# Graph layers on one core: block buffers per graph, key sums taken from w's two parts, t1 and t2 loaded behind the g blocks

## The chip, the cores and the metric

One core of a Trainium2 chip runs the whole problem in one launch. The metric is the time of an execution on the device in microseconds; the median of the runs is compared.

## What is computed

64 graphs of 256 nodes and 512 features pass through two layers in fp32. x and adj are also handed over transposed, and Wv and W1 transposed.

```python
h = jnp.maximum(_layernorm(x, axis=-1), 0.0)
# layer 0, attention weighted by adj
weight = adj * jnp.exp(einsum('bqd,bkd->bqk', h @ Wq.T + bq, h @ Wk.T + bk))
weight = weight / jnp.sum(weight, axis=2, keepdims=True)
x = x + einsum('bqk,bkd->bqd', weight, h @ Wv.T + bv)
# layer 1
h = jnp.maximum(_layernorm(x, axis=-1), 0.0)
agg = einsum('bij,bjf->bif', adj, h) / jnp.maximum(deg, EPS)
x = x + relu(concat([h, agg]) @ W.T)
```

## The kernel before

Graphs are worked in 32 pairs; a pair is 512 rows, four tiles of 128. Each engine has its own program, and semaphores with constant or counted targets bind them. After a first step and step 1 a loop runs steps 2 to 30, then come `last_step` and `final_step`. Step i does layer 0 of pair i and layer 1 of pair j = i - 1, interleaved.

fp32 products are made of three fp32r matmuls (`product`, L514): high by high, high by low, low by high. So every operand X is kept as `X_h` (ACT copies it, L813 to L886) and `X_l` (X minus `X_h`, on POOL or DVE).

PE's step (L660), in order: `kp` (four tiles of the combined query-key projection), `v` tile 0, `scores` of both graphs, `v` 1 to 3; then `strassen` products of layer 1 with weights B11, B21, T1, T2, T3, T4, B22 (p = 0 to 6, two row rounds each), with `az` (adj times z) between them; `sum_weights` (L601: a matrix of ones times the weights' sums over key tiles, so that every partition holds the sum of each query); and four `av`.

Several things share a place. `n_h`/`n_l` hold the kp weights, and, in the middle of a step, t1 and t2 (products 2 and 3): SP loads these after kp (`load_t`, L284) and loads n back after the products (`load_n`, L289). `w` holds adj, then the exponentials and weights of pair i, then u3 and ha1. g_full's memory is that of `g_h` and `g_l`: parts A11, A12 and S4 of h, and u2. All eight PSUM banks are in use and named at L52 to L56.

h must be transposed. DVE turns 32x32 blocks (`turn`, L1072) into `blocks`, SP stores `blocks` to HBM, waits, and loads it back in another order as `turned` (`load_turned`, four DMAs per graph). There is one `blocks` tile, so the second graph's turn waits for the first one's store (L1078, L1085). This happens twice per step: g (layer 1, pair j) and h (layer 0, pair i+1).

DVE ends a step with `sum_ha0`, `layer1_result` for tiles 0 to 3 (y at L1223, then x at L1227) and `sum_inverses` (L1243) before the fourth; then `finish_layer0`. PE's av(t) waits for y of tile t - 1 (L710 to L715), whose bank it takes. POOL's and ACT's last work of a step is hT_h and hT_l of the next pair, then at_h and at_l.

```python
            def sum_weights(i, dst):
                pe.wait_ge(sum_split, i + 1)
                every, all_ones = bank[dst][:, :], ones[:, 0:1].to_broadcast([P, P])
```

## Time and profile before

| | |
|---|---|
| median of 3 runs | 1941.86 us (1937.01 to 1943.64) |
| profiled execution | 1942.48 us, span 1940.4 us |
| PE | busy 98% of the span, 8956 matmuls, mean granted clock 0.996 |
| PE weight loads | 81% |
| DVE, POOL, ACT | 81%, 57%, 44% |
| DMA | 370.7 MB, 191 GB/s |

A row of the timeline gives start, duration, engine and line of an instruction, then what it writes and reads. PE's rows overlap, since a matmul is given with its way through the array; the distance between two starts is what one costs. In the page "idle before" is time in which an engine stood still before an instruction, with what released it.

### The profile page before, as it was taken

How to read it: one execution, taken by the hardware profiler on the slowest of the kernel's cores; microseconds unless marked ns; L12 is line 12 of the kernel's file. 1: busy time of each engine (PE TensorE's matmuls, PEld its weight loads, DVE VectorE, ACT ScalarE, POOL GpSimd, SP SyncE). 2: the span in 40 equal slices, each digit the busy share in tenths (PEclk: the TensorE clock that was granted, in tenths of full speed). 3: DMA queues.
4: the chain of work that ended last, by engine and by line, in shares of the span. 5: the costliest groups of instructions: out<-in, count | busy, mean ns of one | idle time of the engine just before them, and what ended most of it. 6: DMA issues, size and time to landing. Idle time of an engine off the chain costs nothing.

```text
span 1940.4 us, 29261 instructions
## 1 busy us (share of the span) xinstructions
PE 1892.7 (98%) x8956; PEld 1576.8 (81%) x8956; DVE 1579.6 (81%) x2649; ACT 862.4 (44%) x1453; POOL 1103.0 (57%) x1066
## 2 busy tenths in 40 slices
PE   8899999999999999999999999999999999999997
PEld 5778888888888888888788888888888888887885
DVE  6887888888788888888878888887888878888776
ACT  4344444444444445443445443444444454434442
POOL 4665565565565565655655655655655656546552
PEclk9999999999999999999999999999999999999999
DMA  6456656566656566555566555566555665555632
GB/s 222 148 189 212 210 181 196 188 203 207 210 178 190 198 205 204 192 198 173 189 208 219 188 194 184 191 211 211 179 191 194 204 203 194 197 173 184 211 125 87
DMA packets 190881, 370.69 MB, mean 191 GB/s; under 512 B 17936, under 2 KB 115216, under 8 KB 182672
## 3 DMA queue, kind: packets, MB, share of 16 engines
q1 hardware_dynamic: 190864, 370.48, 57.2%
q8 instruction: 9, 0.15, 0.0%
q14 instruction: 8, 0.07, 0.0%
HBM read 266.60 MB, written 103.81 MB: 191 GB/s over the span
## 4 chain that ended last, share of the span: by engine, by line
PE 49%; DVE 19%; DMA 17%; issue 8%; SPq 4%; POOL 2%; ACT 1%; DVEq 1%; POOLq 0%; ACTq 0%
PE bank L518 16%; PE bank L520 16%; PE bank L519 16%; DMA turned_store<-blocks 8%; DMA n_l<-t_store 8%; DVE y L1223 3%; SPq L263 3%; DVE x L1235 3%; DVE stats L1091 2%; DVE x L1227 2%; DVE g_full L1213 2%; DVE deg L1112 1%; DVE mean_sum L1096 1%; DVE blocks L1073 1%; DVE sums L1252 1%
## 5 line engine op out<-in xcount | busy, mean ns | idle before, releaser
L403 POOL TENSOR_TENSOR hT_l<-turned,hT_h 128x512 fp32r<-128x512 f32 x122 | 181.9, 1517 | 264.0 <-ACT hT_h L824 263.9
L242 POOL TENSOR_TENSOR w_l<-w,w_h 128x512 fp32r<-128x512 f32 x62 | 80.3, 1295 | 307.5 <-ACT w_h L857 307.5
L1073 DVE STREAM_TRANSPOSE blocks<-h 128x512 f32<-128x512 f32 x252 | 163.3, 685 | 110.3 <-DMA turned_store<-blocks 110.3
L518 PE MATMUL bank<-hT_h,n_h 128*128 128x512 f32 x512 | 200.9, 392 | 3.9 <-DVE hT_l L1164 2.8
L519 PE MATMUL bank<-hT_l,n_h 128*128 128x512 f32 x512 | 200.2, 391 | 0.0
L520 PE MATMUL bank<-hT_h,n_l 128*128 128x512 f32 x512 | 200.2, 391 | 0.0
L518 PE MATMUL bank<-wv_h,hT_h 128*128 128x512 f32 x512 | 199.6, 390 | 0.0
L519 PE MATMUL bank<-wv_l,hT_h 128*128 128x512 f32 x512 | 199.5, 390 | 0.0
L520 PE MATMUL bank<-wv_h,hT_l 128*128 128x512 f32 x512 | 199.3, 389 | 0.0
L399 POOL TENSOR_TENSOR xb<-x_in,bv_b 128x512 f32<-128x512 f32 x128 | 165.9, 1301 | 43.5 <-DVE x L1235 39.3
L843 ACT ACTIVATE kz_h<-bank,kp_bias 128x512 fp32r<-128x512 f32 x128 | 83.6, 675 | 207.5 <-PE bank L520 207.5
L518 PE MATMUL bank<-hT_h,kz_h 128*128 128x256 f32 x512 | 146.3, 286 | 5.0 <-DVE kz_l L1158 5.0
L519 PE MATMUL bank<-mix_l,g_h 128*128 128x512 f32 x384 | 149.4, 389 | 0.0
L518 PE MATMUL bank<-mix_h,g_h 128*128 128x512 f32 x384 | 149.4, 389 | 0.0
L520 PE MATMUL bank<-mix_h,g_l 128*128 128x512 f32 x384 | 149.4, 389 | 0.0
L818 ACT ACTIVATE h<-x,rs 128x512 f32<-128x512 f32 x124 | 94.4, 809 | 117.0 <-POOL rs L393 117.0
L520 PE MATMUL bank<-hT_h,kz_l 128*128 128x256 f32 x512 | 145.6, 284 | 0.0
L519 PE MATMUL bank<-hT_l,kz_h 128*128 128x256 f32 x512 | 145.6, 284 | 0.0
L1227 DVE SCALAR_TENSOR_TENSOR x<-y,x 128x512 f32<-128x512 f32 x124 | 141.7, 1143 | 4.3
L1123 DVE CUSTOM_DVE_ANT_0 h<-h,u_b,bqk 128x512 f32<-128x512 f32 x128 | 121.4, 968 | 0.0
L518 PE MATMUL bank<-n_h,hT_h 128*128 128x512 f32 x256 | 103.1, 403 | 18.3 <-DMA n_l<-t_store 15.9
L387 POOL TENSOR_TENSOR rs<-var_eps,minus_half 128x2 f32<-128x2 f32 x128 | 90.0, 703 | 50.8 <-DVE var_eps L1101 44.5
(152 smaller groups left out, 5394.9 us busy)
## 6 DMA issues: line engine op xcount, KB each, us to landing
turned_store<-blocks SPq DMA_DIRECT2D x126, 512.0 KB, 4.5
turned<-turned_store SPq DMA_DIRECT2D x504, 128.0 KB, 2.9
x_in<-x SPq DMA_DIRECT2D x32, 1024.0 KB, 5.3
n_h<-t_store SPq DMA_DIRECT2D x31, 1024.0 KB, 6.3
n_l<-t_store SPq DMA_DIRECT2D x31, 1024.0 KB, 8.3
...
```

The costliest lines, as they stand in the source:

```text
L242: engine.tensor_tensor(w_l[:, g], w[:, g], w_h[:, g].bitcast(F32), ALU.subtract).then_inc(w_split, 1)
L387: pool.tensor_tensor(rs[n][:, 0, tiles], var_eps[n][:, tiles], minus_half[:, :], ALU.pow).then_inc(rstd_done[n], 1)
L399: pool.tensor_tensor(xb[:, t, :], x_in[:, t, :], bv_b[:, :], ALU.add).then_inc(xb_done, 1)
L403: pool.tensor_tensor(by_blocks(hT_l, t), turned_tile(t), by_blocks(hT_h, t).bitcast(F32), ALU.subtract).then_inc(hT_split, 1)
L518: pe.matmul(dst, lh, rh, start=first, stop=False, skip_group_check=more)
L519: pe.matmul(dst, lh, rl, start=False, stop=False, skip_group_check=more)
L520: mm = pe.matmul(dst, ll, rh, start=False, stop=last, skip_group_check=more)
L818: nc.scalar.activation(h[:, t, :], src[:, t, :], ACT.Relu, bias=rs[n][:, 1, t:t + 1], scale=rs[n][:, 0, t:t + 1]).then_inc(h_done[n], 1)
L843: nc.scalar.activation(kz_h[:, dt, :], bank[KP_BANK[dt]][:, :], ACT.Identity, bias=kp_bias[:, dt:dt + 1]).then_inc(kp_high, 1)
L1073: nc.vector.transpose(blocks[:, :, :, t % NT, :].rearrange("p j c b -> p c j b"), h[:, t, :].rearrange("p (c j b) -> p c j b", c=DT, b=Q)) ...
L1123: nc.vector.tensor_tensor_reduce(h[:, t, :], h[:, t, :], u_b[:, :], 1.0, bqk[:, 0:1], ALU.mult, ALU.add, key_bias[:, t:t + 1]).then_inc(ke ...
L1227: nc.vector.scalar_tensor_tensor(out=place[:, t, :], in0=y[:, :], scalar=0.0, in1=place[:, t, :], op0=ALU.max, op1=ALU.add).then_inc(x2_do ...
```

## The change

It does six things.

- `blocks` becomes two tiles, one for each graph. A turn waits for the last store of its own tile. On DVE both turns of g stand after the first and second kp split, the degrees behind the kp splits, both turns of h before sum_z.
- SP stores g block 0, issues x_in, stores g block 1, and then loads both. t1 and t2 come behind them in two halves with a semaphore each; PE waits for each half before its own product. `reload_n` puts n_l behind h's store, and h's loads follow when layer 1's parts are made (`parts_made`).
- p0's copies (`z_sum`) move from a tile of their own to g_full's first quarters, the place of A11 and later S4. ACT therefore writes S4 only once z's low parts are made (`z_split`).
- `sum_weights` takes four matmuls, `w_h` and `w_l` by two key tiles, in place of two from `sum_h` and `sum_l`. The pair adds, `high_sum` and `low_sum` go. PE runs them after az(1), in bank 6, instead of after az(3), in bank 7; DVE's `sum_inverses` stands before `sum_ha0`.
- Banks: kp(3) takes 3, v(0) and v(1) 7 and 3, av(0) and av(1) 7 and 1. PE waits for sum_inv before kp(1).
- At the ends W1's feature half is loaded as soon as x1 and the bias sums allow, n's store comes late in the first step, low_mix(T2) stands before hT_l, and the last pair's sum_z and low_z stand before combine_s4 and the degrees.

```diff
-KP_BANK, V_BANK, SCORE_BANK = (5, 6, 2, 7), (3, 7, 0, 1), (0, 1)
-AZ_BANK, AV_BANK, SUM_BANK = (1, 0, 4, 2), (3, 1, 0, 4), 7
+KP_BANK, V_BANK, SCORE_BANK = (5, 6, 2, 3), (7, 3, 0, 1), (0, 1)
+AZ_BANK, AV_BANK, SUM_BANK = (1, 0, 4, 2), (7, 1, 0, 4), 6
...
             wz_raw = (g_full[:, 0], g_full[:, 1])
+            z_sum = (g_full[:, 0, 0, :], g_full[:, 1, 0, :])
             u2 = (g_full[:, 0, 1, :], g_full[:, 1, 1, :])
...
-        blocks = sb("blocks", [P, Q // 8, DT, NT, Q])
+        blocks = [sb(f"blocks{g}", [P, Q // 8, DT, NT, Q]) for g in range(G)]
...
             engine.tensor_tensor(w_l[:, g], w[:, g], w_h[:, g].bitcast(F32), ALU.subtract).then_inc(w_split, 1)
-            engine.wait_ge(w_split, G * i + g + 1)
-            engine.tensor_tensor(w[:, g, 0, :], w[:, g, 0, :], w[:, g, 1, :], ALU.add).then_inc(w_summed, 1)
...
                 sp.dma_start(turned_d[k, g].rearrange("i a j n -> (i a) (j n)"),
-                             blocks[:, :, :, :, :].rearrange("p j c t b -> p (j c t b)")).then_inc(stored[g], 16)
+                             blocks[g][:, :, :, :, :].rearrange("p j c t b -> p (j c t b)")).then_inc(stored[g], 16)
...
-            def move_h(i):
+            def move_g(j, between=None):
+                store_blocks(1, 0, g_turned, T * j + NT, g_stored)
+                if between is not None:
+                    between()
+                store_blocks(1, 1, g_turned, T * (j + 1), g_stored)
                 for g in range(G):
-                    store_blocks(0, g, h_turned, T * (i - 1) + NT * (g + 1), h_stored)
-                    sp.wait_ge(h_stored[g], 16 * i)
-                    load_turned(0, g, h_moved)
-            def move_g(j):
-                for g in range(G):
-                    store_blocks(1, g, g_turned, T * j + NT * (g + 1), g_stored)
                     sp.wait_ge(g_stored[g], 16 * (j + 1))
                     load_turned(1, g, g_moved)
+            def parts_made(j, g):
+                sp.wait_ge(*((combined, 4 * (j + 1)) if g == 0 else (part_split, 7 * j + A22)))
...
-            def load_t(i):
-                sp.wait_ge(kp_psum, DT * (i + 1))
-                sp.dma_start(n_h[:, :, :].bitcast(F32), t_d[0]).then_inc(t_loaded, 16)
-                sp.dma_start(n_l[:, :, :].bitcast(F32), t_d[1]).then_inc(t_loaded, 16)
-            def load_n(j, p):
-                half = slice(2 * (p - 2), 2 * (p - 1))
-                sp.wait_ge(p_psum, PER_PAIR * j + products_done(p, 1))
+            def load_t(k):
+                half = slice(2 * k, 2 * k + 2)
+                sp.dma_start(n_h[:, half, :].bitcast(F32), t_d[0, :, half, :]).then_inc(t_loaded[k], 16)
+                sp.dma_start(n_l[:, half, :].bitcast(F32), t_d[1, :, half, :]).then_inc(t_loaded[k], 16)
+            def reload_n(j, k, h_blocks):
+                half = slice(2 * k, 2 * k + 2)
+                sp.wait_ge(p_psum, PER_PAIR * j + products_done(2 + k, 1))
                 sp.dma_start(n_h[:, half, :].bitcast(F32), n_d[0, :, half, :]).then_inc(n_loaded, 16)
+                sp.wait_ge(h_stored[k], h_blocks)
                 sp.dma_start(n_l[:, half, :].bitcast(F32), n_d[1, :, half, :]).then_inc(n_loaded, 16)
             def load_adj(i):
-                sp.wait_ge(sum_split, i + 1)
+                sp.wait_ge(w_split, G * (i + 1))
                 sp.dma_start(adj_in, adj_d[i]).then_inc(adj_loaded, 16)
...
             def step(i):
                 j = i - 1
-                sp.wait_ge(xb_done, T * (i + 1))
-                load_x(i + 1)
-                move_g(j)
+                def next_x():
+                    sp.wait_ge(xb_done, T * (i + 1))
+                    load_x(i + 1)
+                move_g(j, next_x)
                 if is_first(i):
                     sp.wait_ge(n_stored, 32)
                     sp.wait_ge(t_stored, 64)
-                load_t(i)
+                sp.wait_ge(kp_psum, DT * (i + 1))
+                load_t(0)
+                load_t(1)
                 store_blocks(0, 0, h_turned, T * i + NT, h_stored)
-                load_n(j, 2)
-                load_n(j, 3)
                 store_blocks(0, 1, h_turned, T * (i + 1), h_stored)
-                load_turned(0, 0, h_moved)
-                sp.wait_ge(h_stored[1], 16 * (i + 1))
-                load_turned(0, 1, h_moved)
+                for g in range(G):
+                    reload_n(j, g, 16 * (i + 1))
+                    parts_made(j, g)
+                    load_turned(0, g, h_moved)
                 store_out(j, x1)
                 load_adj(i)
...
                 split_w(pool, i, 0)
                 scale_and_shift(0, i + 1, 0)
                 low_part(j, A11)
                 low_part(j, A12)
                 scale_and_shift(0, i + 1, 1)
-                low_part(j, S1)
-                low_part(j, S3)
                 split_w(pool, i, 1)
-                for m in (S2, A22, S4):
+                for m in (S1, S3, S2, A22, S4):
                     low_part(j, m)
-                low_sum(i)
                 for t in range(T):
                     low_hT(i + 1, t)
...
                 kp(i, 0)
+                pe.wait_ge(sum_inv_done, i)
                 kp(i, 1)
                 if not is_first(i):
                     pe.wait_ge(y_done, T * (i - 1))
                 kp(i, 2)
-                pe.wait_ge(sum_inv_done, i)
                 kp(i, 3)
...
             def sum_weights(i, dst):
-                pe.wait_ge(sum_split, i + 1)
-                every, all_ones = bank[dst][:, :], ones[:, 0:1].to_broadcast([P, P])
-                pe.matmul(every, all_ones, sum_h[:, :, :].rearrange("p g n -> p (g n)"), start=True, stop=False)
-                mm = pe.matmul(every, all_ones, sum_l[:, :, :].rearrange("p g n -> p (g n)"), start=False, stop=True)
+                pe.wait_ge(w_split, G * (i + 1))
+                every = bank[dst][:, :].rearrange("p (g n) -> p g n", g=G)
+                all_ones = ones[:, 0:1].to_broadcast([P, P])
+                for n, part in enumerate((w_h, w_l)):
+                    for c in range(NT):
+                        mm = pe.matmul(every, all_ones, part[:, :, c, :], start=(n == 0 and c == 0),
+                                       stop=(n == 1 and c == NT - 1))
                 mm.then_inc(sum_psum, 1)
...
                 strassen(j, 1, 1)
                 pe.wait_ge(part_split, 7 * j + S1)
-                pe.wait_ge(t_loaded, 32 * i)
+                pe.wait_ge(t_loaded[0], 32 * (j + 1))
                 pe.wait_ge(v_split, T * i + 2)
                 strassen(j, 2, 0)
                 strassen(j, 2, 1)
                 pe.wait_ge(part_split, 7 * j + S2)
+                pe.wait_ge(t_loaded[1], 32 * (j + 1))
                 pe.wait_ge(p0_copied, ROUNDS * j + 1)
...
                 strassen(j, 4, 1)
                 az(j, 1, AZ_BANK[1])
+                sum_weights(i, SUM_BANK)
                 pe.wait_ge(part_split, 7 * j + A22)
...
                 az(j, 3, AZ_BANK[3])
                 pe.wait_ge(ha0_done, ROUNDS * j + 1)
-                sum_weights(i, SUM_BANK)
-                pe.wait_ge(ha0_done, ROUNDS * j + 2)
                 av(i, 0, AV_BANK[0])
+                pe.wait_ge(ha0_done, ROUNDS * (j + 1))
                 pe.wait_ge(y_done, T * j + 1)
                 av(i, 1, AV_BANK[1])
...
-                act.wait_ge(p_psum, PER_PAIR * j + products_done(0, r))
+                act.wait_ge(p_psum, PER_PAIR * j + products_done(0, ROUNDS - 1))
...
                 relu_norm(0, x_in, i + 1, 2)
                 relu_norm(0, x_in, i + 1, 3)
+                act.wait_ge(combined, 4 * j + 3)
+                high_part(j, S2)
                 high_v(i, 3)
-                act.wait_ge(sum_psum, i)
                 copy_p0(j, 0)
                 copy_p0(j, 1)
-                act.wait_ge(combined, 4 * j + 3)
-                high_part(j, S2)
                 high_part(j, A22)
                 high_z(j, 0)
                 high_z(j, 1)
                 act.wait_ge(combined, 4 * j + 4)
-                act.wait_ge(p_psum, PER_PAIR * j + products_done(0, 1))
+                act.wait_ge(z_split, T * j + NT)
                 high_part(j, S4)
                 copy_u2(j, 0)
                 copy_u2(j, 1)
-                act.wait_ge(z_split, T * j + NT)
-                high_sum(i)
-                act.wait_ge(sum_split, i + 1)
+                act.wait_ge(w_split, G * (i + 1))
                 copy_u3(j, 0)
                 copy_u3(j, 1)
...
             def turn(t, done):
-                nc.vector.transpose(blocks[:, :, :, t % NT, :].rearrange("p j c b -> p c j b"),
+                nc.vector.transpose(blocks[t // NT][:, :, :, t % NT, :].rearrange("p j c b -> p c j b"),
                                     h[:, t, :].rearrange("p (c j b) -> p c j b", c=DT, b=Q)).then_inc(done, 1)
             def turn_h(i, g):
                 dve.wait_ge(h_done[0], T * i + NT * (g + 1))
-                if g:
-                    dve.wait_ge(h_stored[0], 16 * i)
+                if not is_first(i):
+                    dve.wait_ge(g_stored[g], 16 * (i - 1))
                 for t in range(NT * g, NT * (g + 1)):
                     turn(t, h_turned)
             def turn_g(j, g):
                 dve.wait_ge(h_done[1], T * j + NT * (g + 1))
-                if g:
-                    dve.wait_ge(g_stored[0], 16 * (j + 1))
+                dve.wait_ge(h_stored[g], 16 * (j + 1))
                 for t in range(NT * g, NT * (g + 1)):
                     turn(t, g_turned)
...
             def layer0(i):
                 j = i - 1
                 low_kp(i, 0)
-                degrees(j)
+                turn_g(j, 0)
                 low_kp(i, 1)
-                dve.wait_ge(h_stored[1], 16 * i)
-                dve.wait_ge(hT_split, T * i)
-                turn_g(j, 0)
+                turn_g(j, 1)
                 low_kp(i, 2)
                 low_kp(i, 3)
-                turn_g(j, 1)
+                degrees(j)
                 low_v(i, 0)
                 weigh(i, 0)
...
                 layer0(i)
                 layer0_stats(i + 1, 0)
-                weigh(i, 1)
-                layer0_stats(i + 1, 1)
-                low_v(i, 1)
                 if not is_first(i):
                     dve.wait_ge(x2_done, T * j)
                 combine_s1(j)
                 combine_s3(j)
+                weigh(i, 1)
+                layer0_stats(i + 1, 1)
+                low_v(i, 1)
                 low_v(i, 2)
-                dve.wait_ge(g_stored[1], 16 * (j + 1))
+                combine_s2(j)
                 turn_h(i + 1, 0)
+                turn_h(i + 1, 1)
                 low_v(i, 3)
-                combine_s2(j)
                 sum_z(j, 0)
                 sum_z(j, 1)
                 low_z(j, 0)
                 low_z(j, 1)
                 combine_s4(j)
-                dve.wait_ge(part_split, 7 * j + A22)
-                turn_h(i + 1, 1)
                 key_bias_of(i + 1, 0)
                 sum_ha1(j, 0)
...
                 low_z(j, 2)
                 key_bias_of(i + 1, 3)
                 low_z(j, 3)
+                sum_inverses(i, SUM_BANK, T * (i + 1) + 1)
                 dve.wait_ge(deg_done, 3 * (j + 1))
                 sum_ha0(j, 0)
                 layer1_result(j, 0, AZ_BANK[0], x1)
                 sum_ha0(j, 1)
                 layer1_result(j, 1, AZ_BANK[1], x1)
                 layer1_result(j, 2, AZ_BANK[2], x1)
-                sum_inverses(i, SUM_BANK, T * (i + 1) + 1)
                 layer1_result(j, 3, AZ_BANK[3], x1)
                 finish_layer0(i, AV_BANK, x1, 16 * (j + 1))
```

How it moves instructions. PE, loop body, from the last product of az(1) on, of the change (`ones` are the key sums' matmuls):

```order
L521 MATMUL bank<-kz_h,at_h 128x512
L522 MATMUL bank<-kz_l,at_h 128x512
L523 MATMUL bank<-kz_h,at_l 128x512
L611 MATMUL bank<-w_h,ones 128x512 x2
L611 MATMUL bank<-w_l,ones 128x512 x2
L521 MATMUL bank<-mix_h,hT_h 128x512
```

Before, the product with T4 followed az(1) at once, and the sums were two matmuls, from sum_h and sum_l, 36 matmuls further on, between az(3) and av(0).

DVE, end of step 1, ordered as the loop's: `kz_l<-bank` is low_z(3), `h<-bank,diagonal` to `sum_inv` sum_inverses, `g_full` sum_ha0, y and x layer1_result. Before, then of the change:

```order
L1213 TENSOR_TENSOR g_full<-bank,g_full 128x512
L1223 SCALAR_TENSOR_TENSOR y<-bank,deg_inv,g_full 128x512
L1227 SCALAR_TENSOR_TENSOR x<-y,x 128x512
L1213 TENSOR_TENSOR g_full<-bank,g_full 128x512
L1223 SCALAR_TENSOR_TENSOR y<-bank,deg_inv,g_full 128x512
L1227 SCALAR_TENSOR_TENSOR x<-y,x 128x512
L1223 SCALAR_TENSOR_TENSOR y<-bank,deg_inv,w 128x512
L1227 SCALAR_TENSOR_TENSOR x<-y,x 128x512
L1249 TENSOR_TENSOR h<-bank,diagonal 128x512
L1252 TENSOR_REDUCE sums<-h 128x4
L1254 RECIPROCAL sum_inv<-sums 128x4
L1223 SCALAR_TENSOR_TENSOR y<-bank,deg_inv,w 128x512
```

```order
L1064 TENSOR_TENSOR kz_l<-bank,kz_h 128x512
L1242 TENSOR_TENSOR h<-bank,diagonal 128x512
L1245 TENSOR_REDUCE sums<-h 128x4
L1247 RECIPROCAL sum_inv<-sums 128x4
L1206 TENSOR_TENSOR g_full<-bank,g_full 128x512
L1216 SCALAR_TENSOR_TENSOR y<-bank,deg_inv,g_full 128x512
L1220 SCALAR_TENSOR_TENSOR x<-y,x 128x512
L1206 TENSOR_TENSOR g_full<-bank,g_full 128x512
L1216 SCALAR_TENSOR_TENSOR y<-bank,deg_inv,g_full 128x512
L1220 SCALAR_TENSOR_TENSOR x<-y,x 128x512
L1216 SCALAR_TENSOR_TENSOR y<-bank,deg_inv,w 128x512
L1220 SCALAR_TENSOR_TENSOR x<-y,x 128x512
```

sum_inverses has moved from behind the third x to behind low_z(3), ahead of all of layer1_result.

DVE, middle of step 1, ordered as the loop's: `y<-y,turned` is combine_s2, `z_full` or `g_full` sum_z, `kz_l` low_z, `v_l` low_v. Before, then of the change:

```order
L1070 TENSOR_TENSOR v_l<-bank,v_h 128x512
L1073 STREAM_TRANSPOSE blocks<-h 128x4x4x32 x2
L1070 TENSOR_TENSOR v_l<-bank,v_h 128x512
L1177 TENSOR_TENSOR y<-y,turned 128x512
L1198 TENSOR_TENSOR z_full<-bank,z_full 128x512 x2
L1070 TENSOR_TENSOR kz_l<-z_full,kz_h 128x512 x2
L1177 TENSOR_TENSOR y<-turned,y 128x512
L1073 STREAM_TRANSPOSE blocks<-h 128x4x4x32 x2
```

```order
L1064 TENSOR_TENSOR v_l<-bank,v_h 128x512 x2
L1170 TENSOR_TENSOR y<-y,turned 128x512
L1067 STREAM_TRANSPOSE blocks<-h 128x4x4x32 x4
L1064 TENSOR_TENSOR v_l<-bank,v_h 128x512
L1191 TENSOR_TENSOR g_full<-bank,g_full 128x512 x2
L1064 TENSOR_TENSOR kz_l<-g_full,kz_h 128x512 x2
L1170 TENSOR_TENSOR y<-turned,y 128x512
```

combine_s2 has moved ahead, and four transposes (both turns of h) and low_v(3) now stand between it and sum_z.

## Rows read from the trace of the kernel before

**Rows 1.** PE's waits, whole span: waiting line, releaser: us in total, times, longest us
```profile
PE bank L518 <- DMA n_l<-t_store: 15.9, 18, 1.5
PE bank L518 <- DVE kz_l L1070: 5.3, 1, 5.3
PE bank L518 <- DVE kz_l L1158: 5.0, 4, 3.6
...
PE bank L518 <- DVE hT_l L1164: 2.8, 1, 2.8
```

**Rows 2.** PE's timeline, where steps begin: start us, us, engine, line, what
```profile
135.34 0.39 PE L518 MATMUL bank<-hT_h,n_h 128*128 128x512 f32 x1
...
1192.47 0.39 PE L518 MATMUL bank<-hT_h,n_h 128*128 128x512 f32 x1
...
1250.43 0.39 PE L518 MATMUL bank<-hT_h,n_h 128*128 128x512 f32 x1
...
1843.43 0.39 PE L518 MATMUL bank<-hT_h,n_h 128*128 128x512 f32 x1
```

**Rows 3.** PE's timeline around the key sums
```profile
1010.10 0.40 PE L604 MATMUL bank<-sum_h,ones 128*128 128x512 f32 x1
...
1010.57 0.39 PE L518 MATMUL bank<-v_h,w_h 128*128 128x512 f32 x1
```

**Rows 4.** SP's queue, timeline of the step from 1016.04: issues
```profile
1027.05 0.37 SPq L251 DMA_DIRECT2D x_in<-x  x1
1028.92 0.34 SPq L258 DMA_DIRECT2D turned_store<-blocks  x1
1033.67 1.76 SPq L263 DMA_DIRECT2D turned<-turned_store  x4
...
1040.77 0.43 SPq L286 DMA_DIRECT2D n_h<-t_store  x1
```

**Rows 5.** DVE's and POOL's timelines in the last pair
```profile
1910.39 1.76 DVE L1177 TENSOR_TENSOR xb<-turned,xb 128x512 f32<-128x512 f32 x1 [1.19 <-POOL hT_l L408]
...
1910.32 1.28 POOL L408 TENSOR_TENSOR hT_l<-turned,hT_h 128x512 fp32r<-128x512 f32 x1
```

**Rows 6.** Timelines of ACT, DVE, POOL and PE, end of that step
```profile
1063.29 0.60 ACT L813 ACTIVATE kz_h<-bank 128x512 fp32r<-128x512 f32 x1 [0.76 <-PE bank L520]
...
1066.23 0.69 DVE L1227 SCALAR_TENSOR_TENSOR x<-y,x 128x512 f32<-128x512 f32 x1
...
1068.45 1.43 DVE L1227 SCALAR_TENSOR_TENSOR x<-y,x 128x512 f32<-128x512 f32 x1
1069.98 0.75 DVE L1223 SCALAR_TENSOR_TENSOR y<-bank,deg_inv,w 128x512 f32<-128x512 f32 x1
...
1071.49 0.68 DVE L1249 TENSOR_TENSOR h<-bank,diagonal 128x512 int32<-128x512 int32 x1
...
1072.93 0.18 DVE L1254 RECIPROCAL sum_inv<-sums 128x4 f32<-128x4 f32 x1
...
1073.93 1.70 DVE L1227 SCALAR_TENSOR_TENSOR x<-y,x 128x512 f32<-128x512 f32 x1
...
1066.52 6.20 POOL L403 TENSOR_TENSOR hT_l<-turned,hT_h 128x512 fp32r<-128x512 f32 x4 [8.20 <-ACT hT_h L824]
1072.68 2.40 POOL L426 TENSOR_TENSOR at_l<-adjT,at_h 128x1024 fp32r<-128x1024 f32 x1
...
1073.11 0.39 PE L518 MATMUL bank<-v_h,w_h 128*128 128x512 f32 x1
```

**Rows 7.** Timelines of POOL, DVE and PE, middle of that step
```profile
1045.32 1.30 POOL L408 TENSOR_TENSOR hT_l<-y,hT_h 128x512 fp32r<-128x512 f32 x1
...
1045.82 1.30 DVE L1073 STREAM_TRANSPOSE blocks<-h 128x512 f32<-128x512 f32 x2
...
1051.43 2.55 DVE L1070 TENSOR_TENSOR kz_l<-z_full,kz_h 128x512 fp32r<-128x512 f32 x2 [0.54 <-ACT kz_h L813]
...
1054.93 0.39 PE L518 MATMUL bank<-kz_h,at_h 128*128 128x512 f32 x1
```

144 lines of the change are left out of this document (68 added, 76 removed).

## The prediction

> **What bounds the kernel now.** I read the page's busy shares, PE's waits, PE's timeline, then SP's and the other engines' timelines of one middle step (1016.04 to 1074.47 us; every time below without another origin is in it). PE is busy in 98% of the span, so time is matmuls plus gaps. Its waits [rows 1] name one recurrent gap: 15.9 us in 18 pieces on `n_l<-t_store`, the load of t1 and t2. The others are nearly all at the ends: 5.3 us on kz_l (L1070) in the last pair, 2.8 us on hT_l before pair 1's projections, 3.6 of the 5.0 us on kz_l (L1158) before pair 1's scores. Waits count less than they cost, since a matmul's row overlaps the next start. Step starts show it all [rows 2]: a step without a gap takes 1250.43 - 1192.47 = 57.96 us, the 29 steps from 135.34 to 1843.43 take 58.90 on average. So the loop holds 29 x 0.94 = 27.3 us of gaps. That is all a better order can win there; every new matmul costs its start-to-start time.
>
> **Part by part.**
>
> Key sums: two matmuls per pair become four of the same width. The two of before, from 1010.10 to 1010.57 [rows 3], take 0.235 us each, start to start. 64 more: **+15.0 us**, on PE, covered by nothing. A second bound is the 0.227 us of the other 512-wide ones (14.5 us). The Trainium skill (TensorE: Matmul & The Clock Gate, Part 1) has 215.7 ns for 512 columns at 2.4 GHz; by it the term would be 13.8 us. The trace disagrees by 0.02 us each and decides.
> POOL's pair adds and low_sum, and ACT's high_sum go: no gain in the loop, because PE never waited for sum_l there; in the first step one wait on it goes, counted with the ends.
>
> t1 and t2: before, SP stores g block 0, waits for it, loads it, does the same with block 1, and only then issues t at 1040.77 [rows 4]. With two block buffers DVE turns block 0 right after the first key projection and block 1 after the second. The first store is then issued at about 1026.1 instead of 1028.92, x_in (1027.05) behind it, the second store at about 1028.1, and SP waits at 1033.4 at the latest for both (x_in and one store together took from 1027.05 to 1033.67, 6.6 us, and the loads of block 0 are issued meanwhile). The four loads of block 1, 0.44 us each, put t's issue at about 1035.5. That is 5 us earlier, and t1 goes ahead of t2. PE wants t1 24 matmuls before az(0), whose row is at 1054.93 [rows 7], so at 1049.5. I take all 0.94 us per step of gap as gone: **-27.3 us** (bound: the other small waits in the loop stay, -25).
>
> p0 in A11's place: the copies go to g_full, so S4 may be written only after z's low parts. The cost is order, not work.
>
> Ends: W1's first half is loaded before x of pair 1, low_sum leaves POOL's chain, and in the last pair sum_z stands ahead of combine_s4 and the degrees. The waits on hT_l (2.8) and kz_l (3.6, and 5.3 at the end) [rows 1] with the slower clock behind them are 12 to 20 us; I take **-12**, bounds 0 and -18.
>
> **What takes the gain back: one lock, met at two new places.** When DVE adds two operands from SBUF while POOL works, DVE waits for POOL's instruction. At 1910.39 combine_s4 came just after the POOL operation that released it, but the next POOL operation (1910.32 to 1911.60) was already in: it ended at 1912.15, 0.55 us behind that [rows 5]. At 1073.93 x<-y,x met at_l (1072.68 to 1075.08) and ended at 1075.63, again 0.55 behind [rows 6]. The Trainium skill (SBUF — State Buffer, SBUF: two separate sides) calls this an exclusive lock held for the whole instruction. Taken literally the loser would end 0.69 us, a full x<-y,x, behind the winner; the row says 0.55. By the page the stall below is 0.14 us longer per step, 4 us in all.
>
> End of a step. Both orders hang on high_z(3), which ends at 1063.89 [rows 6]. DVE before: low_z, then g_full at 1064.65, x at 1066.23, 1068.45, y for t=2 at 1069.98. Now sum_inverses (1071.49 to 1073.11, 1.6 us) stands first, so the first x<-y,x comes at about 1067.8. ACT before waited for the h blocks until 1065.8; now reload and moves come earlier and ACT writes hT_h right behind high_z(3). POOL's four hT_l (1.3 each, start to start 1.26) then run from 1064.5, the third to 1068.3. x meets it and ends at 1068.85; the fourth hT_l ends 1.15 later, at 1070.0, and at_l (2.4) starts there. The next x<-y,x arrives 1.53 us after the first one's end (1066.92 to 1068.45 before), at 1070.4: 0.4 us too late. It waits until 1072.4 and ends at 1072.95; y for t=2 follows, to 1073.8. av(3), at 1073.11 before, would be due 0.47 earlier (the sums now stand ahead of high_z(3)), at 1072.64, and waits for that y: **1.2 us per step**, about 1.3 with the restart. Before, at_l met only the fourth x, on which nobody waited. Since the second x always comes one fixed stretch after the POOL operation that held the first, the meeting doesn't depend on small shifts. 30 steps: +39.
>
> Middle of a step. The g blocks land at about 1037.6, just when POOL begins A11's and A12's low parts (1.3 each). combine_s1, combine_s3 and weigh(1), 0.7 us each, all read two operands from SBUF and alternate with them: done at 1041.7, where alone they would be done at 1039.7. Then DVE's statistics (1.8), POOL's rs (1.3), split_w (1.3) and S1 (1.3) follow each other, and S1, which ended at 1046.6 before [rows 7], ends at 1047.3. combine_s2 waits for S1 and meets S3 just as combine_s4 met its neighbour in [rows 5]: done at 1049.15. Now four transposes (0.65 each [rows 7]; two of them stood behind combine_s4 before) and low_v precede sum_z: z's second low part ends at about 1054.85, against 1053.98 before. az(0) began at 1054.93 after 0.47 us of gaps, so 1054.46 is due: 0.4 us late. Behind it combine_s4 (0.7), high_part S4 (0.6) and copy_u2 (0.6) reach st T3 0.4 us late too. **0.8 us per step**, 0.9 with restarts: +27 for 30 steps; bounds 0 (blocks land 1 us earlier, before A11) and 1.8.
>
> Other moved steps, at nothing. Ahead of low_kp(2), for which PE's scores wait, DVE has degrees (1.7) out and the second turn (1.3) in. PE's new place for sum_inv's wait, before kp(1), comes 13 us after sum_inverses. SP's reload of n_l waits for h_stored, and h's loads behind it, yet they land some 2 us before ACT wants them; if that cover went, hT_l would be late for the next kp. Out's stores keep their place behind x2.
>
> Sum against the profiled execution, 1942.5 us (span 1940.4 and 2.1 around it; the median of the runs is 1941.9, the same): 1942.5 + 15.0 - 27.3 - 12 + 39 + 27 = 1984. I allow 3 us for steps in which one meeting is missed: **1981 us**.
>
> **Rivals.**
> A. The end-of-step meeting alone; the middle has enough slack. For it: the middle's chain is eight steps long, and its lateness at each of two places only 0.4 us. 1942.5 + 15 - 27.3 - 12 + 39 = 1957. Chance 0.26.
> B. Neither meeting: the change does what its words say, PE runs without gaps, and only the sums are paid. 1942.5 + 15 - 27.3 - 12 = 1918: faster. It decides on where the second x stands against at_l: if POOL's hT_l start 0.5 us later (h blocks later than 1064), or the first x slips in before the third hT_l, y is ready at 1071.9 and av(3) has 0.7 us to spare. For it: x arrives only 0.4 us behind at_l's start. Against: h's moves have about 2 us in hand. Chance 0.24.
> C. The middle alone: 1945. Chance 0.08.
> D. t1 and t2 still come late, since SP waits for both stores before any load: PE keeps part of the 27 us. An issue at 1035.5 and a landing within 8 us against a need at 1049.5 speak against it. Half of the 27 us left on top of the forecast: 1981 + 14 = 1995. Chance 0.02.
>
> **How the numbers follow.** My forecast (both meetings) has 0.40. A measurement of this kernel can tell 0.3%, 5.8 us, from no change. Faster is B and a rare part of C: 0.24. Same is most of C, and A where the meeting costs half: 0.10. Slower is forecast, A and D: 0.66. The range drops B and keeps the rest with the bounds of the ends (0 to -18) and of the middle: 1936 to 1998.
>
> **What would show it.** Right: 128 matmuls of the sums at 0.235 us; no wait on `t_store`; steps of about 60.5 us; PE waiting on DVE y (layer1_result) 1.1 us or so before av(3) in most steps, with x<-y,x of some 2.5 us beside at_l; PE waiting on kz_l and on g_full's copies in the middle. Wrong: steps of 58.4 us (B), y waits alone and steps of 59.7 (A), or PE waiting for `t_store` (D). In the ends, kp of pair 1 should start near 66 us (68.9 before), and the 5.3 us wait at the end should halve.

## The result and the profile after

| | us |
|---|---|
| before, median of 4 runs | 1940.7 (1937.0 to 1943.6) |
| after, median of 4 runs | 1995.7 (1994.7 to 1997.2) |
| ratio | 1.0285, 95% interval 1.0265 to 1.0305 |
| profiled execution after | 1996.7, span 1994.9, mean granted clock 0.997 |
| predicted | 1981 (1936 to 1998) |

The change makes the kernel 55 us slower. The page of the changed kernel, busy time and the chain that ended last:

```profile
PE 1933.0 (97%) x9020; PEld 1579.7 (79%) x9020; DVE 1514.9 (76%) x2647; ACT 843.6 (42%) x1421; POOL 957.4 (48%) x972
...
issue 32%; PE 21%; DVE 21%; POOL 20%; ACT 3%; DMA 1%; POOLq 1%; DVEq 1%; SPq 0%; ACTq 0%
```

DVE and POOL have less to do than before (76% for 81, 48% for 57), DMA has left the chain (1% for 17), and the kernel is slower: the chain now passes through DVE and POOL for 41% of the span. What PE waits for (line, releaser: us in total, times, longest us), beside [rows 1]:

```profile
PE bank L521 <- DVE kz_l L1064: 13.4, 30, 0.5
PE bank L521 <- DVE y L1216: 11.7, 11, 1.3
PE bank L521 <- ACT g_full L873: 9.6, 16, 0.7
...
PE bank L611 <- DVE v_l L1064: 3.0, 1, 3.0
PE bank L521 <- DVE kz_l L1151: 2.4, 2, 1.4
PE bank L521 <- POOL hT_l L416: 1.9, 2, 1.4
```

No row names t_store any more. In its place stand three waits on other engines: for z's low part before az(0), for y before av(3), and one before the product with T2, which the view puts down to the copies of p0 (L873). The middle of a step, below, shows that this third one is for another operand. The first row of pair 1's kp, of step 2, of a step without the wait on y, of the one after it, and the first behind the 30th step, in PE's timeline (start us, us, engine, line, what), beside [rows 2]:

```profile
70.94 0.39 PE L521 MATMUL bank<-hT_h,n_h 128*128 128x512 f32 x1
...
132.87 0.39 PE L521 MATMUL bank<-hT_h,n_h 128*128 128x512 f32 x1
...
499.65 0.39 PE L521 MATMUL bank<-hT_h,n_h 128*128 128x512 f32 x1
...
559.30 0.39 PE L521 MATMUL bank<-hT_h,n_h 128*128 128x512 f32 x1
...
1902.19 0.39 PE L521 MATMUL bank<-hT_h,n_h 128*128 128x512 f32 x1
```

The 29 steps from 132.87 to 1902.19 take 61.01 us on average (58.90 before), the shortest 59.65. That is 61.2 us more in the loop. Outside it the change gains 6.8: pair 1 begins 2.1 us later (70.94, 68.88 before), step 1 takes 61.9 us for 66.5, and what follows the loop 92.7 for 97.0. 61.2 - 6.8 = 54.4, the difference of the spans (54.5).

Adding up in both traces by how much each matmul starts later than its usual distance behind the last (0.227 us for 512 columns, 0.234 for the sums) gives the gaps of a step, mean of the 29:

| gap in front of | before | after |
|---|---|---|
| product with T1 or T2 | 0.83 | 0.58 |
| az(0) | 0 | 0.72 |
| product with T3 | 0 | 0.37 |
| av(2), av(3) | 0 | 0.62 |
| scores, next kp | 0.08 | 0.21 |
| sum | 0.91 | 2.50 |
| step without its gaps | 57.99 | 58.51 |

A gap is longer than its wait. The rows of the wait before az(0) in the step from 1352.52:

```profile
1392.69 0.50 PE L521 MATMUL bank<-kz_h,at_h 128*128 128x512 f32 x1 [0.45 <-DVE kz_l L1064]
1393.04 0.40 PE L522 MATMUL bank<-kz_l,at_h 128*128 128x512 f32 x1
```

The matmul that waited takes 0.50 us for 0.39, and the next starts 0.35 us behind it instead of 0.23: 0.11 us of restart. Another 0.16 us is lost without being counted as a wait, because the matmul before is still shown as running (0.39 us) when the next would have started (0.23). So a wait of 0.45 us is a gap of 0.72.

**The end of a step.** The meeting that was predicted is there, in about a third of the steps. In the step from 1352.52 (62.87 us), ACT, DVE, POOL and PE:

```profile
1406.39 1.15 ACT L833 ACTIVATE hT_h<-turned 128x512 fp32r<-128x512 f32 x2 [2.24 <-DMA turned<-turned_store]
...
1410.57 2.41 DVE L1220 SCALAR_TENSOR_TENSOR x<-y,x 128x512 f32<-128x512 f32 x1
1413.08 0.75 DVE L1216 SCALAR_TENSOR_TENSOR y<-bank,deg_inv,w 128x512 f32<-128x512 f32 x1
...
1410.04 2.40 POOL L434 TENSOR_TENSOR at_l<-adjT,at_h 128x1024 fp32r<-128x1024 f32 x1
...
1413.89 0.50 PE L521 MATMUL bank<-v_h,w_h 128*128 128x512 f32 x1 [1.28 <-DVE y L1216]
```

The second x<-y,x arrives 0.53 us after at_l has begun, ends 0.54 behind it (the 0.55 of [rows 5]), and av(3) waits 1.28 us. By the exclusive lock of the Trainium skill (SBUF — State Buffer, SBUF: two separate sides), taken literally, it would be a whole x<-y,x behind, 0.69; the trace has 0.54 here too. One step later (from 1415.38, 59.74 us):

```profile
1470.80 1.15 ACT L833 ACTIVATE hT_h<-turned 128x512 fp32r<-128x512 f32 x2 [4.56 <-DMA turned<-turned_store]
...
1471.43 0.69 DVE L1220 SCALAR_TENSOR_TENSOR x<-y,x 128x512 f32<-128x512 f32 x1
1472.22 0.75 DVE L1216 SCALAR_TENSOR_TENSOR y<-bank,deg_inv,w 128x512 f32<-128x512 f32 x1
...
1474.95 2.86 POOL L434 TENSOR_TENSOR at_l<-adjT,at_h 128x1024 fp32r<-128x1024 f32 x1
```

Here the second graph's blocks of h land 55.4 us into the step and not 53.9 (ACT waits 4.56 us for them). POOL reaches at_l at 59.6 us of the step and not at 57.5, the second x<-y,x is through in 0.69 us, and PE doesn't wait. This step has no gap before av(2) and av(3), where the one before has 2.1 us. All 29 steps sort this way: in the nine in which ACT gets the second graph's blocks 52.7 to 53.9 us into the step, the gap on y is 1.3 us or more; in the twenty with 54.3 to 56.9 us it is 0.6 at most.

**The middle of a step**, the one from 1352.52:

```profile
1381.53 0.69 POOL L400 TENSOR_TENSOR rs<-var_eps,minus_half 128x2 f32<-128x2 f32 x1 [3.71 <-DVE var_eps L1094]
...
1382.72 1.31 POOL L239 TENSOR_TENSOR w_l<-w,w_h 128x512 fp32r<-128x512 f32 x1
1383.98 1.30 POOL L421 TENSOR_TENSOR hT_l<-y,hT_h 128x512 fp32r<-128x512 f32 x1
...
1387.81 1.29 POOL L421 TENSOR_TENSOR hT_l<-y,hT_h 128x512 fp32r<-128x512 f32 x1 [1.29 <-ACT hT_h L869]
...
1385.32 1.75 DVE L1170 TENSOR_TENSOR y<-y,turned 128x512 f32<-128x512 f32 x1 [1.74 <-POOL hT_l L421]
1386.99 2.48 DVE L1067 STREAM_TRANSPOSE blocks<-h 128x512 f32<-128x512 f32 x4
...
1387.10 0.63 ACT L869 ACTIVATE hT_h<-y 128x512 fp32r<-128x512 f32 x1 [1.91 <-DVE y L1170]
1387.64 0.58 ACT L822 ACTIVATE v_h<-bank 128x512 fp32r<-128x512 f32 x1
1388.12 1.08 ACT L873 ACTIVATE g_full<-bank 128x512 f32<-128x512 f32 x2
...
1389.23 0.49 PE L521 MATMUL bank<-n_h,hT_h 128*128 128x512 f32 x1 [0.54 <-ACT g_full L873]
```

DVE waits 1.74 us for S1's low part, combine_s2 (L1170) meets S3's low part and takes 1.75 us for 0.69, four transposes follow. ACT waits 1.91 us for combine_s2, makes S2's high part and only then copies p0 (L873), whose product has long been done; POOL makes S2's low part meanwhile. The product with T2 needs S2's low part and, for its first row round, only the first of the two copies. That copy has 0.5 us in hand. PE starts at 1389.23, 0.13 us behind the end of S2's low part (1387.81 and 1.29), and this distance is 0.13 us in each of the 29 steps. The second copy, needed a round later, merely happens to end last before the start, and so the view names it. The wait before T2 is therefore one for S2's low part, and behind it for combine_s2. And POOL, before S1, waits 3.71 us for a variance while w_h, which it could have split, is ready at 1380.36. Three queues each hold ready work behind a wait; which of them cost time, the runs have to show.

### The profile page after: what moved, and what is told of

Same layout as the page of the kernel before. It is cut to its first block, busy times and chain, and to the rows that moved or that the text cites. A ratio compares the mean times of both kernels' runs of the same rounds, so it can differ in the third digit from the quotient of the medians.

```text
span 1994.9 us, 29325 instructions
## 1 busy us (share of the span) xinstructions
PE 1933.0 (97%) x9020; PEld 1579.7 (79%) x9020; DVE 1514.9 (76%) x2647; ACT 843.6 (42%) x1421; POOL 957.4 (48%) x972
## 4 chain that ended last, share of the span: by engine, by line
issue 32%; PE 21%; DVE 21%; POOL 20%; ACT 3%; DMA 1%; POOLq 1%; DVEq 1%; SPq 0%; ACTq 0%
PE bank L521 7%; PE bank L523 6%; PE bank L522 6%; POOL xb L412 6%; DVE y L1216 4%; POOL rs L400 3%; DVE x L1220 3%; POOL hT_l L421 3%; POOL g_l L421 3%; POOL w_l L239 2%; DVE kz_l L1064 2%; DVE g_full L1206 2%; DVE blocks L1067 2%; ACT kz_h L822 2%; DVE h L1116 1%
## 5 line engine op out<-in xcount | busy, mean ns | idle before, releaser
L416 POOL TENSOR_TENSOR hT_l<-turned,hT_h 128x512 fp32r<-128x512 f32 x122 | 168.7, 1405 | 315.9 <-ACT hT_h L833 315.9
L1220 DVE SCALAR_TENSOR_TENSOR x<-y,x 128x512 f32<-128x512 f32 x124 | 137.5, 1109 | 4.3
L1200 DVE TENSOR_TENSOR w<-bank,w 128x512 f32<-128x512 f32 x64 | 44.1, 691 | 107.8 <-ACT w L877 107.8
L521 PE MATMUL bank<-kz_h,at_h 128*128 128x512 f32 x256 | 103.3, 403 | 14.3 <-DVE kz_l L1064 13.4
```

Source lines behind the costliest of these rows:

```text
L416: pool.tensor_tensor(by_blocks(hT_l, t), turned_tile(t), by_blocks(hT_h, t).bitcast(F32), ALU.subtract).then_inc(hT_split, 1)
L521: pe.matmul(dst, lh, rh, start=first, stop=False, skip_group_check=more)
L1220: nc.vector.scalar_tensor_tensor(out=place[:, t, :], in0=y[:, :], scalar=0.0, in1=place[:, t, :], op0=ALU.max, op1=ALU.add).then_inc(x2_do ...
```

## The experiments

Twelve kernels in three groups; the kernels of a group ran on one chip, each group on another. The kernel before took 1937.7 us on the first chip, 1919.0 on the second, 1949.7 on the third. The changed kernel (1995.7 and 1995.0) and the kernel of e6 and e11 (1918.8 and 1919.6) agree between chips within 0.8 us, so the changed kernel's relatives are compared by their times; why before doesn't agree is a subject of e9.

### e1 and e2: what the four sum matmuls cost

e1, eight matmuls of 256 contiguous columns:

```
-    every = bank[dst][:, :].rearrange("p (g n) -> p g n", g=G)
+    for g in range(G):
+        own = bank[dst][:, g * nodes:(g + 1) * nodes]
...
-            mm = pe.matmul(every, all_ones, part[:, :, c, :], ...
+            mm = pe.matmul(own, all_ones, part[:, g, c, :], ...
```

> The changed kernel with its key sums taken graph by graph: eight matmuls of 256 contiguous columns in place of four whose moving operand is two pieces of 256 columns that lie 512 elements apart. In the changed kernel each of the four takes 0.341 us from start to start where other 512-wide matmuls take 0.227. Theory 1, the two-piece operand is what costs the extra 0.114 us: the eight take 0.12 us each (the start-to-start time of 256-wide matmuls in this trace), 0.96 us a step for 1.36, which is 32 times 0.40 = 13 us less, about 1983 us. Theory 2, the extra time belongs to each matmul on the ones (its weights or what reads w at that time), not to the shape: each of the eight takes 0.12 + 0.11, 1.87 us a step, 32 times 0.51 = 16 us more, about 2012 us.

Measured: 1998.8 us. e2, another layout of w's parts:

```
-w_h, w_l = sb("w_h", [P, G, NT, nodes], F32R), ...
+w_h, w_l = sb("w_h", [P, NT, G, nodes], F32R), ...
-            mm = pe.matmul(every, all_ones, part[:, :, c, :], ...
+            mm = pe.matmul(every, all_ones, part[:, c].rearrange("p g n -> p (g n)"), ...
```

> The changed kernel with w's high and low parts laid out with the key tile outside the graph, so that each of the four sum matmuls reads 512 contiguous columns; the copies that write w_h and w_l now write two pieces. Theory 1 (two-piece operand): each of the four back at 0.23 us, 0.92 us a step for 1.36, 32 times 0.44 = 14 us less, about 1982 us. Theory 2 (the ones or the time of the read): still 0.34 us each, 1996 us. If the strided writes cost ACT, DVE or POOL more, w_h<-w rises above 0.632 us and w_l<-w,w_h above 1.29 us.

Measured: 1996.5 us. Both theories fall, because the number they explain was misread: I had set the sums' 0.234 us against the 0.120 of 256-wide matmuls and booked the rest as extra. The rows of the changed kernel, two matmuls to a row, with the matmul behind them:

```profile
1032.62 0.63 PE L611 MATMUL bank<-w_h,ones 128*128 128x512 f32 x2
1033.08 0.62 PE L611 MATMUL bank<-w_l,ones 128*128 128x512 f32 x2
1033.54 0.39 PE L521 MATMUL bank<-mix_h,hT_h 128*128 128x512 f32 x1
```

0.46 us for two, 0.92 for four. In e1:

```profile
1033.29 0.39 PE L612 MATMUL bank<-w_h,ones 128*128 128x256 f32 x2
1033.52 0.39 PE L612 MATMUL bank<-w_l,ones 128*128 128x256 f32 x2
```

0.23 for two halves. So four or eight matmuls, of contiguous columns or of two pieces, take the same, and the prediction's 0.235 us was right.

### e3: the inverses of the key sums back in their place

```
 key_bias_of(i + 1, 3); low_z(j, 3)
-sum_inverses(i, SUM_BANK, T * (i + 1) + 1)
...
 layer1_result(j, 2, AZ_BANK[2], x1)
+sum_inverses(i, SUM_BANK, T * (i + 1) + 1)
 layer1_result(j, 3, AZ_BANK[3], x1)
```

> The changed kernel with one thing undone on VectorE: the inverses of the key sums (1.6 us of three instructions) stand again behind the third result of layer 1 and not ahead of all four. Theory 1, the wait ahead of the last av is VectorE's chain to the second and third y, which the inverses pushed back into the time of POOL's at_l: av(3)'s waits of 1.2 to 1.9 us in about 10 of 29 steps go, 10 times 1.5 = 15 us less, about 1981 us, and at most 0.2 us of wait on y is left in any step. Theory 2, the same lateness is handed on: the next step's second kp matmul group waits for the inverses instead, with waits of about 1 us on sum_inv, and the time stays at 1994 to 1998 us.

Measured: 1982.5 us, 13 us less. Its waits:

```profile
PE bank L521 <- ACT g_full L873: 13.5, 25, 0.7
PE bank L521 <- DVE kz_l L1064: 13.4, 30, 0.5
PE bank L521 <- DVE kz_l L1151: 7.4, 13, 1.4
```

The waits on y are gone, and theory 1 holds in size; part of the lateness is handed on as theory 2 had it, to another place: DVE reaches the next pair's kz_l (L1151) late, and PE waits for it before the scores (0.30 us of gap a step for 0.10). The wait before T2 comes more often (25 times for 16).

### e4: the middle, two moves

```
 relu_norm(0, x_in, i + 1, 3)
+copy_p0(j, 0); copy_p0(j, 1)
 act.wait_ge(combined, 4 * j + 3)
 high_part(j, S2); high_v(i, 3)
-copy_p0(j, 0); copy_p0(j, 1)
...
 low_v(i, 2)
+turn_h(i + 1, 0)
 combine_s2(j)
-turn_h(i + 1, 0)
 turn_h(i + 1, 1)
```

> The changed kernel with two moves in the middle of a step: ScalarE copies p0 ahead of the high part of S2 (it stands idle there for 1.9 us), and VectorE turns the first graph's two tiles of h ahead of combine_s2 (it stands idle there for 1.7 us). Theory 1, the middle waits come from those two queues' order: the wait ahead of az(0) (0.5 us plus 0.11 of restart in every step), those on copy_p0 (0.3 to 0.9 in two thirds of the steps) and on copy_u2 (0.26 plus 0.11) go, 1.2 to 1.6 us a step, 30 times that = 36 to 48 us less, 1948 to 1960 us. Theory 2, VectorE's chain is held by POOL's low part of S1 and the meeting of combine_s2 with POOL's low part of S3: only the wait on copy_p0 goes, 30 times 0.5 = 15 us less, about 1981 us, and az(0) still waits.

Measured: 1964.6 us, 31 us less: between the theories. The gaps before az(0) (0.72) and T3 (0.37) are gone, 1.09 x 29 = 32 us; the one before T2 stayed (0.66 us a step, 0.58 in the changed kernel), and the view now names another releaser:

```profile
PE bank L521 <- POOL hT_l L421: 12.7, 22, 0.7
PE bank L521 <- DVE y L1216: 11.5, 14, 1.3
```

The second copy now ends 3 us before T2 starts, and T2 still starts 0.13 us behind S2's low part in every step, as it did in the changed kernel. Making the copies earlier has bought nothing there, and both theories had expected it to. POOL is late with S2 because S1's low part was late. No run separates the two moves for az(0) and T3; in the changed kernel ACT waits 0.97 us for DVE's sum_z before it makes z's high parts (1390.68), which speaks for the transposes.

### e5: POOL splits w before it waits for the variance

```
 low_part(j, A12)
+split_w(pool, i, 1)
 scale_and_shift(0, i + 1, 1)
-split_w(pool, i, 1)
```

> The kernel of e4_mid (1964.6 us) with one more exchange: POOL makes the low part of w of the second graph ahead of the scale and shift of layer 0's second half, which in the trace it waits 0.7 to 1.4 us for while w_h has long been there. Theory 1, the waits of 0.7 to 0.86 us ahead of the product with T2 that e4_mid kept in 22 steps come from POOL's low part of S2, at the end of the queue w_l, S1, (combine_s2), S2: with w_l 1.3 us earlier S1's low part starts 0.7 us earlier and the wait goes, 0.56 + 0.1 us a step in the mean, 30 times that = 17 to 20 us less, 1945 to 1948 us. Theory 2, combine_s2 then meets the low part of S3 for longer (it ends with it, whenever it starts), and S2 comes no earlier: 1962 to 1966 us.

Measured: 1953.0 us, 11.6 less than e4. The gap before T1 and T2 falls from 0.66 to 0.13 us a step, as theory 1 had it, and a quarter of that comes back at the end of the step, where PE, now earlier, waits for y more:

```profile
PE bank L521 <- DVE y L1216: 18.3, 16, 1.3
```

### e6: the inverses in a stretch in which DVE waits

```
 key_bias_of(i + 1, 1); key_bias_of(i + 1, 2)
+sum_inverses(i, SUM_BANK, T * (i + 1) + 1)
 low_z(j, 2); key_bias_of(i + 1, 3); low_z(j, 3)
-sum_inverses(i, SUM_BANK, T * (i + 1) + 1)
```

> The kernel of e5_swap with VectorE's inverses of the key sums (1.6 us) in the stretch in which it waits for z's third high part, behind the third key bias. Theory 1, the end of the step is VectorE's chain from the sums of the last product to y of t=2, and the inverses stand in it: taken out, all waits ahead of av(3) (0.57 + 0.11 us a step in the mean in e4_mid) and those of the scores behind it (0.1 to 0.2) go, 30 times 0.75 = 20 to 24 us less than e5_swap, 1922 to 1928 us, below the kernel before (1938 to 1941). Theory 2, the meeting of x<-y,x with POOL's at_l is what decides, and comes about wherever VectorE stands: the waits on y stay near 0.4 us a step, 1935 to 1945 us.

Measured: 1918.8 us, 34 less than e5, 77 less than the changed kernel. Its page and its steps:

```profile
PE 1894.7 (99%) x9020; PEld 1588.7 (83%) x9020; DVE 1559.9 (81%) x2647; ACT 843.5 (44%) x1421; POOL 961.9 (50%) x972
...
PE 94%; DVE 4%; issue 1%; DMA 0%; ACT 0%; SPq 0%; POOL 0%; DVEq 0%
```
```profile
130.44 0.39 PE L521 MATMUL bank<-hT_h,n_h 128*128 128x512 f32 x1
...
1824.41 0.39 PE L521 MATMUL bank<-hT_h,n_h 128*128 128x512 f32 x1
```

29 steps of 58.41 us with 0.01 us of gap in each. I had expected 20 to 24 us, but e5 still held 1.04 us of gap a step, 0.81 on y and 0.1 on the scores behind it, and all but 0.01 went. Theory 2 is refuted by a step in which the meeting takes place:

```profile
1353.88 0.75 DVE L1216 SCALAR_TENSOR_TENSOR y<-bank,deg_inv,w 128x512 f32<-128x512 f32 x1
1354.67 1.91 DVE L1220 SCALAR_TENSOR_TENSOR x<-y,x 128x512 f32<-128x512 f32 x1
...
1353.18 2.85 POOL L434 TENSOR_TENSOR at_l<-adjT,at_h 128x1024 fp32r<-128x1024 f32 x1
...
1357.21 0.39 PE L521 MATMUL bank<-hT_h,n_h 128*128 128x512 f32 x1
```

x<-y,x takes 1.91 us beside at_l, but it is the third, and y for t=2 was made before it. Over the whole span x<-y,x takes 1.28 us on average here and 1.11 in the changed kernel: more meetings, and none that PE sees.

### e7 and e8: two sum matmuls in the loop instead of four

Both make the sum of w over the key tiles on DVE and split it on ACT and POOL, as before, into A12's place (g_h and g_l), with the sum matmuls ahead of az(0). e7 does it to the changed kernel, e8 to e6's:

```
+sum_h, sum_l = (a[:, 1, :].rearrange("p (g n) -> p g n", g=G) for a in (g_h, g_l))
...
+def high_sum(i):
+    act.wait_ge(w_summed, G * i)
+    act.wait_ge(p_psum, PER_PAIR * (i - 1) + products_done(1, 1))
+    nc.scalar.activation(sum_h, w[:, :, 0, :], ACT.Copy).then_inc(sum_high, 1)
```

> The changed kernel with the key sums of the loop made as before from a sum of w over the key tiles with its high and low parts (two matmuls for four; VectorE's two additions, ScalarE's and POOL's splits in stretches in which those engines wait, the parts in A12's place, the matmuls ahead of az(0)). Theory 1, the four matmuls cost the 0.47 us a step that two more take: 30 times 0.47 = 14 us less, about 1982 us, if the added work (0.7 + 0.7 us of VectorE, 0.6 of ScalarE, 1.3 of POOL) stays hidden. Theory 2, the time of PE does not bound, since PE waits 2.5 us a step for the other engines, and the added work lengthens exactly those chains: no gain or a loss, 1995 to 2025 us.

> The kernel of e6_slot with the key sums of the loop in two matmuls, as in e7_oldsum, the additions and splits in VectorE's, ScalarE's and POOL's waiting stretches of that kernel's order. Theory 1, with the waits gone PE's own time bounds, and two matmuls less a step are worth their 0.47 us: 30 times 0.47 = 14 us below e6_slot, about 1912 us. Theory 2, the added work brings back the wait ahead of the product with T2 or ahead of az(0), 0.3 to 0.8 us a step: no gain or up to 10 us above e6_slot.

Measured: e7 1968.2 us, 27 less than the changed kernel, where 14 or none were expected; e8 1942.0, 23 more than e6. e8 is clear: PE waits for S2's low part in every step, since ACT may write the sum into A12's place only when A12's product is done, and copies p0 (L897) and makes S2's high part behind it. Its waits, and ACT's queue in one step:

```profile
PE bank L531 <- POOL hT_l L423: 27.9, 31, 0.9
```
```profile
1052.37 0.63 ACT L890 ACTIVATE g_h<-w 128x512 fp32r<-128x512 f32 x1 [1.10 <-PE bank L533]
1052.90 1.06 ACT L897 ACTIVATE g_full<-bank 128x512 f32<-128x512 f32 x2
```

In e7 the same wait (27.4 us, 31 times) covers the one before az(0), and the gaps on y fell to 0.09 us a step while those of the next kp on hT_l rose from 0.11 to 0.35: the h blocks come later there, and at_l with them. Its gain is 0.47 us a step of matmuls and 0.6 of gaps, and it doesn't price the matmuls alone.

### e9, e10 and e11: the same kernels on one more chip

> The kernel before, once more, on the chip of this group of runs (the second group's chip gave it 1919 us, the first's 1938 and the recorded runs 1941). Theory 1, what differs is the wait of the product with T1 on t_store's landing, 0.83 us a step in the recorded profile (27 us in all): on a chip with 1919 us the waits on t_store sum to 5 to 10 us and the rest of PE's times is the same to 0.5%; on one with 1940 us they sum to 25 to 30. Theory 2, such a chip runs everything faster (matmuls from start to start under 0.227 us): the waits on t_store sum to more than 25 us there too.

> The changed kernel, once more, beside the kernel before on the same chip. It has no wait on t_store and its waits are those of VectorE, ScalarE and POOL, so by theory 1 (the chips differ in how late the loads land) it takes 1990 to 1999 us on any of them, and the ratio is 1.028 where the kernel before takes 1940 and 1.039 where it takes 1919. By theory 2 (the whole chip is faster) the ratio stays 1.028: 1973 us beside 1919.

> The kernel of e6_slot, once more, beside the kernel before and the changed kernel. PE has no wait in its loop, so no chip should change it: 1917 to 1921 us. Where the kernel before takes 1940, the ratio is 0.989; where it takes 1919, 1.000. Against the changed kernel on the same chip 0.960 to 0.965 (theory 1 of e10_after).

Measured on one chip: e9 1947.6 us (12 runs; the group's own runs of the kernel before 1949.7), e10 1995.0, ratio 1.0244 (1.0226 to 1.0261), e11 1919.6, ratio 0.9845 (0.9832 to 0.9857). e9's waits, beside [rows 1]:

```profile
PE bank L518 <- DMA n_l<-t_store: 20.8, 22, 1.6
```

The waits on t_store rose from 15.9 to 20.8 us and the loop from 58.90 to 59.10 us a step, while a step without its gaps stays at 57.99. I had given 25 to 30 us of waits for a chip with 1940; with the restarts the gaps before the products with T1 and T2 are 29 us here and 24 in the recorded profile, so the expectation's sizes were gaps, not waits. Theory 1 is borne out: what differs between these two occasions is how late t lands (n_l 8.9 us from issue, 8.3 in the recorded profile), and e10 and e11, which have no such wait, take the times that their kernels took before, so the whole chip isn't slower (theory 2). The kernel before wasn't profiled on the chip where it took 1919 us; that the wait is almost absent there is only concluded from the time.

### e12: the sums' parts in a place that is free earlier

```
-sum_h, sum_l = (a[:, 1, :].rearrange(...) for a in (g_h, g_l))
+sum_h, sum_l = (a[:, 2, :].rearrange(...) for a in (kz_h, kz_l))
...
 high_part(j, S3)
+high_sum(i)
...
+low_part(j, S1)
+low_sum(i)
+for m in (S3, S2, A22, S4):
```

> The kernel of e6_slot with two sum matmuls in the loop in place of four, again from a sum of w and its split, but with the parts in the third tile of kz, free from the scores on, and POOL's part of it ahead of S3 (in e8_best the parts stood in A12's place, ScalarE could write them only after the product with A12, and S2's low part came 0.9 us late in every step). Theory 1: the waits of e8_best came from that place, and two matmuls less are worth 0.47 us a step: 30 times 0.47 = 14 us below e6_slot, 1904 to 1908 us. Theory 2: the added 0.7 + 0.7 us of VectorE, 0.6 of ScalarE and 1.3 of POOL don't fit ahead of S2 in any place: waits of 0.3 to 0.9 us a step ahead of the product with T2 or of az(0), 1915 to 1930 us.

Against e6's kernel e12 also copies the second half of p0 behind S2's high part, and against e8 it runs the sum matmuls behind az(1) again. Measured: 1921.5 us, 2 more than e11 and 20 less than e8. That fits theory 1 on the place, though place, order and matmuls changed together; on the sum theory 2 is right:

```profile
PE bank L530 <- POOL hT_l L423: 3.3, 15, 0.5
```

The steps take 58.44 us, of which 0.42 are gaps, 0.3 before T2 and 0.11 before T3. Two matmuls less give 0.46 us a step, and the gaps, which come with 2 us more of POOL and ACT ahead of S2, take nearly all of it back. The version that is best on both chips is e6's: 1918.8 against 1919.0 on the chip where before is fastest (ratio 0.9998, 0.9989 to 1.0007), 1919.6 against 1949.7 where it is slowest.

## Why the prediction was right, and where it wasn't

Slower was given 0.66 and the forecast 1981 us; it came to 1995.7, near the top of the range. The range is looser than it looks: its upper end doesn't follow from the bounds given (the middle's 1.8 us a step alone would make 1981 + 27 = 2008). The nearest single time was rival D's 1995, and the traces exclude D, so the time alone wouldn't have told the forecast from it. By the prediction's own terms, measured over the 29 steps and the ends of the profiled execution:

| term | predicted | measured |
|---|---|---|
| two more sum matmuls a step | +15.0 | +15.1 (13.3 the two matmuls, 1.8 gaps too small to place) |
| the loop's gaps of before | -27.3 | -26.4 |
| end of a step | +39 (30 x 1.3) | +24.1 (18.0 on y, 6.1 on kp and scores) |
| middle of a step | +27 (30 x 0.9) | +48.4 (20.9 az(0), 10.7 T3, 16.8 T2) |
| ends | -12 | -6.8 |
| a missed meeting | -3 | in the end's term |
| sum | 38.7 | 54.4 |

**The sums** came out as predicted (15.1 is what a step without its gaps grew, 0.52 us, times 29; the predicted 15.0 counts all 32 pairs at 0.47). Two matmuls are 0.46 of the 0.52: e6's steps without gaps take 58.41 us, those of before 57.96; e1 and e2 show that the shape of the operand has no part in it.

**The loads of t1 and t2** are early enough: no wait names t_store, though they are issued 21.1 us into the step (median) and not 19.5; rival D is out, and the -27.3 is the one gain that came as predicted. What it is worth depends on the chip: the kernel before ranges over 31 us between chips.

**The end of a step** was right in mechanism (sum_inverses ahead, x<-y,x held by at_l to 0.54 us behind its end, y for t=2 late, 1.3 us before av(3)) and wrong in how often. The step that failed is "the meeting doesn't depend on small shifts": I let DVE's first x and POOL's fourth hT_l hang on the same event, high_z(3). Behind it stands the premise that h's loads "land some 2 us before ACT wants them". They don't: in every step ACT, done with the first graph's copies, waits for the second graph's blocks, 1.4 to 5.2 us, 3.7 in the median. So the third and fourth hT_l, and at_l behind them, hang on a landing. Only the nine steps with the earliest landings have a gap on y of 1.3 us or more, where the prediction expected it in most. Rival B had named the condition (later blocks) and was put aside because of those 2 us. e3 bears out the part of the inverses: the waits on y go by undoing that alone, 13 us net of what comes back before the scores and T2.

**The middle** was under-estimated. az(0) (predicted 0.4 late, measured 0.61 late and 0.11 of restart) and T3 (0.4, measured 0.37 in all) are there. What was put at nothing is T2: I took the whole 0.94 of old gap as gone. In e6, without gaps, T2 starts 35.7 us into a step. S2's low part is ready at 36.2 (median of the 29). The prediction's chain would have made it in time: it has combine_s2 done at 1049.15, 33.1 us into its step, and the changed kernel has it done at 34.2. The lateness is there from the start of the chain. POOL begins A11's low part 22.4 us into the step and not at 21.6, and ends S1's at 32.4 and not at 31.3. So the step that failed here is the timing of that chain, which left T2 out. That is +16.8 us, more than the whole error of the sum. e5 is the test: with POOL's exchange S1's low part ends at 31.3, combine_s2 at 33.1, and the gap falls to 0.13 us. ACT's copies of p0 are not the cause, as e4 shows. In all, the two moves of e4 and the exchange of e5 take 43 us away, and what they change is the order in the queues around combine_s2.

**The ends**: pair 1 begins at 70.94 and not near 66. PE's sum matmuls of pair 0 wait 3.0 us for DVE, a wait that the direct sums put in the place of 1.5 us on sum_l. The wait of 5.3 us in the last pair is gone, but step 1 and the tail give only 8.9 us together.

The two big terms err in opposite ways, -15 and +21. That the sum comes within 15 us is in part luck: had the end of a step erred upwards by the same 15 us, the time would have been about 2025 us, outside the range.
